# Graph layer on one Trainium2 core: two of six early expert tiles moved from behind the edge loop into it

## What is computed

```python
xf = layernorm(x)                                  # 3125 x 256
gate_logits = xf @ Wg + bg                         # 8 experts
top_w, top_i = top_k(gate_logits, 2)
w = softmax(top_w)                                 # two experts for each node
for e in range(8):                                 # 256 -> 1024 -> 256
    h = gelu(xf @ W1[e] + b1[e])
    out = out + w_dense[:, e:e+1] * (h @ W2[e] + b2[e])
return x + out
```

## Time and profile before

| | |
|---|---|
| median of three runs | 973.71 us (973.17 to 973.80) |
| the profiled execution | 970.97 us |
| its span, first to last instruction | 968.9 us |
| mean granted TensorE clock | 0.916 of full |
| busy: PE, DVE, ACT, POOL | 83%, 55%, 44%, 58% |
| the chain that ended last | PE 39%, POOL 26%, issue 15%, DVE 10%, DMA 6% |

### The profile page before, as it was taken

The page is one execution under the profiler, slowest core; times in us unless marked ns, Lnnn a source line. Parts: engine busy times, 40 slices in busy tenths (PEclk is TensorE's granted clock), DMA queues, the critical chain, the costliest instruction groups (busy, mean ns, idle before and its releaser), DMA issues.

```text
span 968.9 us, 17802 instructions
## 1 busy us (share of the span) xinstructions
PE 801.5 (83%) x4831; PEld 693.5 (72%) x4832; DVE 531.3 (55%) x1485; ACT 424.4 (44%) x1125; POOL 565.6 (58%) x580
## 2 busy tenths in 40 slices
PE   7986676776765557978798777799999999999995
PEld 6885554554554446867687665699999999999994
DVE  6789787887776787667677768741111111111111
ACT  4656433443353235774755662543333333333330
POOL 2077777777777777777777777365333333333331
PEclk8997899779677778997999899799999999999998
DMA  8347554555456445756665674973656656656652
GB/s 237 112 127 236 141 135 137 139 155 139 124 156 196 131 127 150 246 171 190 197 178 145 177 229 116 301 238 62 195 163 184 195 162 190 189 165 191 186 162 22
DMA packets 80183, 162.18 MB, mean 167 GB/s; under 512 B 11569, under 2 KB 46278, under 8 KB 79989
## 3 DMA queue, kind: packets, MB, share of 16 engines
q1 hardware_dynamic: 49029, 91.06, 28.9%
q0 software_dynamic: 30528, 69.83, 28.4%
q10 hardware_dynamic: 560, 0.52, 0.2%
HBM read 144.12 MB, written 17.25 MB: 167 GB/s over the span
## 4 chain that ended last, share of the span: by engine, by line
PE 39%; POOL 26%; issue 15%; DVE 10%; DMA 6%; DVEq 1%; ACT 1%; POOLq 0%; ACTq 0%
POOL gathered L999 24%; PE bank L1714 12%; PE bank L1734 12%; PE bank L1563 4%; PE bank L1380 2%; DMA gathered<-h_table,src_row 2%; DVE gathered L2016 2%; DVE acc L1985 2%; PE bank L1620 2%; DMA out<-one_hot 1%; PE bank L1644 1%; PE bank L1550 1%; DMA w_sb<-in_L_gnn_att_dst 1%; DVEq L1979 1%; PE bank L1702 1%
## 5 line engine op out<-in xcount | busy, mean ns | idle before, releaser
L999 POOL DMA_INDIRECT gathered<-h_table,src_row x416 | 402.2, 967 | 129.0 <-issue 126.0
L1563 PE MATMUL bank<-gathered,one_hot 128*128 128x260 f32 x832 | 248.3, 450 | 133.0 <-DVE acc L1985 131.0
L1563 PEld LDWEIGHTS bank<-gathered,one_hot 128*128 128x128 f32 x832 | 174.8, 221 | 179.3 <-DVE acc L1985 149.5
L1345 ACT ACTIVATE one_hot<-bank,one_hot 128x128 f32<-128x128 f32 x312 | 89.2, 369 | 182.5 <-PE bank L1714 182.5
L1059 POOL DMA_INDIRECT out<-one_hot x39 | 61.2, 1569 | 168.8 <-DMA out<-one_hot 114.4
L1714 PEld LDWEIGHTS bank<-one_hot,acc 128*128 128x128 f32 x1248 | 145.5, 192 | 2.7 <-ACT one_hot L1337 0.8
L1714 PE MATMUL bank<-one_hot,acc 128*128 128x128 f32 x1248 | 145.9, 275 | 0.5 <-ACT one_hot L1337 0.5
L1734 PE MATMUL bank<-w_sb,one_hot 128*128 x624 | 141.1, 379 | 0.0
L2016 DVE TENSOR_TENSOR gathered<-gathered,bank 128x1024 f32<-128x1024 f32 x104 | 127.0, 1221 | 3.5 <-ACT gathered L1203 0.4
L1985 DVE TENSOR_TENSOR acc<-acc,bank 64x260 f32 x208 | 87.9, 423 | 70.1 <-issue 53.5
L1734 PEld LDWEIGHTS bank<-w_sb,one_hot 128*128 128x128 f32 x624 | 115.6, 190 | 14.3 <-issue 0.2
(11 more groups left out here) (363 smaller groups left out, 1009.5 us busy)
## 6 DMA issues: line engine op xcount, KB each, us to landing
acc<-in_L_ffn_W SPq DMA_DIRECT2D x40, 1024.0 KB, 5.1
w_sb<-in_L_ffn_W SPq DMA_DIRECT2D x16, 1024.0 KB, 11.4
w_sb<-key_table SPq DMA_DIRECT2D x52, 256.0 KB, 3.5
gathered<-h_table,src_row POOLq DMA_INDIRECT x416, 3.1
h_table<-acc SPq DMA_DIRECT2D x25, 130.0 KB, 2.2
xs<-in_L_ffn_W SPq DMA_DIRECT2D x3, 1024.0 KB, 11.2
out<-xs SPq DMA_DIRECT2D x5, 512.0 KB
xn_table<-w_sb SPq DMA_DIRECT2D x5, 512.0 KB, 5.3
```

The lines of the kernel that those rows point to most:

```text
L999: pool.indirect_dma_start(gathered[:, r, j, :], None, h_table, bass.IndirectOffsetOnAxis(ap=src_row[:, t:t + 1], axis=0)).then_inc(gather_ ...
L1345: op = act.activation(hiddenT[:, k, g * P:(g + 1) * P], hidden_bank[2 * k + half][:, f * P:(f + 1) * P], ACT.Gelu, bias=b1_slot[:, k, g:g ...
L1563: mm = pe.matmul(sum_bank[r % SUMS][:, 0:ROW], one_hot[:, r, j, :], gathered[:, r, j, :], start=(j == 0), stop=(j == G - 1))
```

## The change

The first two of expert 0's three early tiles run inside the edge loop as tiles 10 and 11 of now NI = 12; four (one of expert 0, three of expert 1) are left behind it (NA = 4). All tiles in the loop begin one group sooner, tile 11 at step 99, so that its narrow is in the last step, 103. The weights of expert 0's first layer are loaded at q = 47 instead of behind the loop. `early_work` does two steps in each group. The dynamic tiles are the same.

```diff
-NA = FIRST * DEPTH
+FA = FIRST * DEPTH
+XA = 2
+NA = FA - XA
...
+NI = NL + XA
-FIRST_TURN = 56
+FIRST_TURN = 55
-FIRST_ROWS = 57
+FIRST_ROWS = 56
-EVENTS = 3 * NL + 1
+EVENTS = 3 * NI + 1
...
-        xg_a = [xs[:, 16 + u, :] for u in range(4)] + [xs[:, 8 + u, :] for u in range(2)]
+        xg_a = [xs[:, 16 + u, :] for u in range(4)] 
...
@@ SP, in the edge loop
+                        if q == 47:
+                            computed(c, 24)
+                            sp.dma_start(b2_first, b2[0:1, :]).then_inc(wa_in, 16)
+                            sp.dma_start(w1_a[0], layer_one(0)).then_inc(wa_in, 16)
...
                         if q == 51:
                             computed(c, 30)
+                            sp.wait_ge(wa_in, c * 48 + 33)
+                            sp.sem_inc(waited, 1)
                             sp.dma_start(w2_a[0], layer_two(0)).then_inc(wa_in, 16)
...
@@ SP, behind it
-                    computed(c, 24)
-                    sp.dma_start(w1_a[0], layer_one(0)).then_inc(wa_in, 16)
...
@@ POOL: early_rows_in, and behind the loop
+                    if u == NL:
+                        pool.wait_ge(early_step, c * EARLY_OPS + EARLY_OPS)
+                        pool.sem_inc(waited, 1)
+                        for k in range(2):
+                            pool.wait_ge(xn_stored[k], c * ((len(BATCHES) + 1 - k) // 2 * 16) + 33)
+                            pool.sem_inc(waited, 1)
...
-                for u in range(4, NA):
-                    read_early(u)
...
-                for u in range(8, NL):
+                for u in range(8, NI):
                     add_rows(u)
...
@@ ACT, step
-                    early_gelu(c, s)
-                    if s == EARLY_AT + 5:
+                    if s == EARLY_AT + 3:
                         act.wait_ge(early_step, c * EARLY_OPS + LIST_OPS + 12)
                         act.activation(powers, powers, ACT.Exp).then_inc(powers_ready, 1)
+                    early_gelu(c, s)
...
@@ PE, in the loop
-                        if part == 1 and u and u % LD == 0:
+                        if part == 1 and u == NL:
+                            other_weights(c, 32)
+                        elif part == 1 and 0 < u < NL and u % LD == 0:
...
+                    if u == NL:
+                        other_weights(c, 48)
...
-                        mm = pe.matmul(y_l, hidden_l[:, g * P:(g + 1) * P], w2_l[:, g, :], start=False, stop=(g == KF - 1))
+                        mm = pe.matmul(y_l, hidden_l[:, g * P:(g + 1) * P], (w2_l if u < NL else w2_a[0])[:, g, :], start=False, stop=(g == KF - 1))
...
@@ PE, behind the last put
-                for u in range(DEPTH, NA):
-                    if u > DEPTH:
-                        early_widen(u, 0)
-                        early_widen(u, 1)
-                    if u + 1 < NA:
-                        if u + 1 == 4:
-                            pe.wait_ge(xga_in[1], 16 * (NA - 4))
-                        early_turn(u + 1)
-                    early_narrow(u - 1, 0)
-                    early_narrow(u - 1, 1)
+                pe.wait_ge(experts_ready, 1)
+                early_narrow(2, 0)
+                early_narrow(2, 1)
...
@@ DVE, step
-                    early_work(c, s)
+                    for k in range(2):
+                        early_work(c, 2 * (s - EARLY_AT) + k)
```

More of the change, by code:

```diff
@@ L77 @@
 EARLY_OPS = LIST_OPS + 30
[L78 removed]
+EVENTS = 3 * NI + 1
 WEIGHTS = 208
[L80 removed]
+MINPAIRS = -(-(2 * N - (NA + NI) * P) // (2 * P))
 SPARE = P
@@ L961, in add_rows @@
                         pool.wait_ge(y_added, u * 16)
-                    pool.indirect_dma_start(out, bass.IndirectOffsetOnAxis(ap=add_l[:, u:u + 1], axis=0),
+                    where = add_l[:, u:u + 1] if u < NL else add_a[:, u - NL:u - NL + 1]
+                    pool.indirect_dma_start(out, bass.IndirectOffsetOnAxis(ap=where, axis=0),
                                             rows_l[u], None, compute_op=ALU.add).then_inc(y_added, 16)
@@ L1210, in rows_out @@
                     products(c, 3 * u + 4)
-                    act.activation(rows_l[u], y_l, ACT.Copy, scale=share_l[:, u:u + 1]).then_inc(scalar_l, 1)
+                    own = share_l[:, u:u + 1] if u < NL else share_a[:, u - NL:u - NL + 1]
+                    act.activation(rows_l[u], y_l, ACT.Copy, scale=own).then_inc(scalar_l, 1)
                 def early_parts(c, s):
@@ L1217, in early_parts @@
                     u, part = (s - FIRST_TURN) // PERIOD, (s - FIRST_TURN) % PERIOD
-                    if part == 0 and 1 <= u <= NL:
+                    if part == 0 and 1 <= u <= NI:
                         rows_out(c, u - 1)
-                    if part == 0 and 0 <= u < NL:
+                    if part == 0 and 0 <= u < NI:
                         products(c, 3 * u + 2)
@@ L1225, in early_gelu @@
                     u, part = (s - FIRST_TURN) // PERIOD, (s - FIRST_TURN) % PERIOD
-                    if part == 2 and 0 <= u < NL:
+                    if part == 2 and 0 <= u < NI:
                         products(c, 3 * u + 3)
-                        at = (LOW + u // LD) * KF
+                        at = (LOW + u // LD) * KF if u < NL else 0
                         for g in range(KF):
@@ L1297, in early_gelu @@
                         g = half * (KF // 2) + f
-                        op = act.activation(hidden_a[:, u % 2, g * P:(g + 1) * P], bank[5 + (2 * u + half) % 3][:, f * P:(f + 1) * P], ACT.Gelu,
-                                            bias=b1_cols[:, u // DEPTH * KF + g:u // DEPTH * KF + g + 1])
+                        op = act.activation(hidden_a[:, u % 2, g * P:(g + 1) * P], bank[5 + (2 * (u + XA) + half) % 3][:, f * P:(f + 1) * P], ACT.Gelu,
+                                            bias=b1_cols[:, (u + XA) // DEPTH * KF + g:(u + XA) // DEPTH * KF + g + 1])
                     op.then_inc(hidden_ready, 1)
@@ L1326, in _ @@
                 shares(8)
-                for u in range(DEPTH, NA):
+                for u in range(3, NA):
                     for half in range(2):
@@ L1513, in weights, with other_weights @@
                     pe.sem_inc(waited, 1)
+                def other_weights(c, count):
+                    pe.wait_ge(wa_in, c * 48 + count + 1)
+                    pe.sem_inc(waited, 1)
                 def early_products(c, s):
@@ L1519, in early_products @@
                     u, part = (s - FIRST_TURN) // PERIOD, (s - FIRST_TURN) % PERIOD
-                    if part == 0 and 1 <= u <= NL:
+                    if part == 0 and 1 <= u <= NI:
                         early_narrow_in(c, u - 1)
-                    if not 0 <= u < NL:
+                    if not 0 <= u < NI:
                         return
@@ L1614, in early_widen @@
                         pe.wait_ge(hidden_ready, 2 * u + half - 2)
-                    if u == DEPTH and half == 0:
+                    if u + XA == DEPTH and half == 0:
                         pe.wait_ge(wb_in, 32)
@@ L2185, in after_step @@
                         dve.sem_inc(waited, 1)
-                    step = s - EARLY_AT
                     if step == 0:
```

74 lines of the change are left out of this document (37 added, 37 removed).

## The result

The changed kernel takes 992.23 us (median of 4 executions, 991.35 to 994.69) against 973.75: ratio 1.0191, 95% interval 1.0168 to 1.0215. Slower, as forecast; 986.8 was too low, the range held it. The profiled execution took 991.76 us with a span of 990.0 us, 21.1 more than the span of before (968.9).

A forecast was written before the change was run, and what follows sets the result against it. POOL bounds the edge loop, PE the tiles from about 704 us; between them PE and POOL's chain of adds arrive together. Terms 1.1 + 5.5 + 3.5 + 1.5 + 1.5 = +13.1 us gave 986.8 us, range 977 to 995.

The forecast's parts named there:

- Covered edits ... All at 0: Weight loads, early list work, early exponential and SP order, all moved sooner, cost 0, with +2 in the range.
- Two gathers on POOL, +1.1: Edge loop: two more tiles' gathers cost POOL 2.5 us, moving the last exponentials by +1.1, between 0 and +2.5.
- The loop's end, +5.5: Loop's end: the twelfth tile's gelus and narrow in series make exponentials to last add 12.3 us instead of 6.8.
- POOL waits for the gelu, +3.5: Behind the loop: add 0 waits for the twelfth gelu, later adds meet weight loads, delaying `put` 0; 0 to +7.
- PE does the same as now: Before the last `put`, PE's work stays as before: widen 0 to 3, narrow 0 and 1.
- A colder PE, +1.5: PE idles 5 us before `put` 0 and restarts slowly once: +1.5, bounds 0 and 2.8.
- Removal worth nothing, +1.5 for the tail: After the routing: two tiles fewer gain nothing because POOL's adds keep their length; contended loads cost +1.5, between 0 and +4.
- Every new wait restarts PE at the lower clock: Rival: waits at `put` 0, first and third dynamic transpose cost 2.8 us each; +20, 993.7 us, chance 0.13.
- Only the loop's end shifts: Rival: adds land undisturbed, `put` 0 waits for nothing, PE stays warm; +6.6, 980.3 us, chance 0.20.
- faster: Rival: earlier weight loads shorten the adds before tile 5's gather, which lands 6.6 us sooner; -2.2, 971.5 us, chance 0.11.
- The signs: Dynamic row gather 10 to 13 us later, POOL waiting 9 us, last sums near 608, PE idle at two places.

The follow-up runs named there:

- run 1: The changed kernel with the early tiles' row gathers one group later in POOL's program, as in the kernel before; 6.3 us faster than the changed kernel.
- run 2: The kernel before with its ten early tiles begun one group sooner, transposes and row gathers, no extra tile; 5.8 us slower than the kernel before.
- 8: The changed kernel with row gathers one group later, adds unwaited and spread, last narrow behind the last sums, two dynamic gathers early; 970.57 us, ratio 0.9965.
- 9: All four edits together, plus early tile 1's widen reading expert 0's weights instead of expert 1's; not faster than the four edits' 970.57 us.
- number 10: All four edits together, plus PE's narrow of early tile 0 ahead of early tile 1's widen; not faster than the four edits' 970.57 us.
- run 11: The kernel before with adds 7, 8 and 9 spread over POOL's weaves and the first early add before tile 0's gather; some 2 us slower.
- run 12: The changed kernel without the two extra loop tiles, first tile at its old place, four early tiles behind; 3.4 us slower than the kernel before.
- Run 4: The changed kernel with the twelfth tile's narrow behind the last edge sums and its rows copy behind the deviations and normalisations; 993.49 us.
- 5: The changed kernel with the row gathers for dynamic tiles 2 and 3 moved behind adds 9 and 10; 5.6 us slower than the changed kernel.
- 7: The changed kernel with adds early and 7 to 11 spread over weaves, two dynamic gathers earlier; last put to dynamic turn 5 38.96 us instead of 51.82.
- run 3: The changed kernel without POOL's waits for the last early tile ahead of the adds; some 2 us less than the changed kernel.

## Why the prediction was right in sign and too low

- **The failed step is "Covered edits ... All at 0".** Beginning one group sooner was costed by what PE, DVE and SP do with it; the row gather on POOL, the engine that bounds the loop, moved ahead of its list. The price is at least one group of POOL's gathers (5.0 us): undoing it gives 6.3 us in run 1, and doing it alone costs 5.8 to 6.6 in run 2, where 3.1 us of the profiled execution's loss lie behind the loop. The trace of the kernel before told it: 344.07 with a wait of 0.40 in the kernel before, 1.28 us after the list's last operation.
- *Two gathers on POOL, +1.1:* neither refuted nor measured. From row gather to A it is 250.2 to 250.9 us in runs 1, 8, 9 and 10 (twelve tiles, gather at group 57), and 249.5, 247.3 and 250.3 in the kernel before and runs 11 and 12 (ten tiles, the same group): the scatter of the three is larger than the term. In runs 1, 8, 9 and 10 the list itself is done 1.5 to 2.5 us later than in the kernel before; why is open (run 11, with the old loop, shows +0.8 too).
- *The loop's end, +5.5:* the series was right, the sum mis-sized: +7.20, in every run with the narrow inside the loop. Left out was the second half of the twelfth tile's widen, which stands on PE ahead of the gelus (the table load waits 1.24 us for it). Run 4 takes bias row, narrow and rows copy out: 5.07 of it.
- *POOL waits for the gelu, +3.5:* half the story; +5.45 (the prediction's own chain of adds gave 3.1, and 3.5 was taken). The adds alone would hold `put` 0 by as much (run 4), but so does a second chain that I denied ("PE does the same as now"): early tile 1 is now one of expert 1, whose first-layer weights go into the accumulators' space and start only after the last scaling (SP issues them at 623.35, behind the stores of the last node tiles). Alone it costs 4.3 us in A to C and 3.4 us of the kernel (run 12).
- *A colder PE, +1.5:* +1.62 in C to D. The half widen behind `put` 0 took 3.39 us instead of 1.96. That the size fits C to D is in part luck: in run 1 `put` 0 waits 2.85 us, the half widen behind it takes 1.96, and C to D is 22.31 as in the kernel before. There the slow stretch comes behind a wait of 1.46 us at the first dynamic tile (half widens of 2.81 and 2.66 us instead of 2.05 and 1.95), and D to E is 53.52.
- *Removal worth nothing, +1.5 for the tail:* right. D to E +0.10, the rest +0.96, and runs 5, 7, 11 and 12 show it from four sides: with seven adds between the last `put` and the first dynamic add 51.5 to 53.8 us, with or without the two tiles; with five adds and the tiles 51.35; with four adds and without the tiles 39.0 (in runs 9 and 10, with more adds delayed, 39.2 and 40.5).
- *Rivals.* "Every new wait restarts PE at the lower clock" lay nearest, at 993.7, but not for its reason. At its three places PE ran a half widen in 3.39 instead of 1.96 us behind a wait of 2.93, the first half widen of a dynamic tile in 2.05 behind 1.41, as in the kernel before, and a narrow in 5.40 instead of 3.62 behind 11.17: 3.2 us in all, where that rival had 8.4. The windows view of the changed kernel shows the granted clock of the stretches with the first and the other two waits, and between them one without a wait (busy us of PE, PEld, DVE, ACT, POOL; clock, a mean of the two levels 1.2 and 2.4 GHz; DMA, GB/s):

```profile
645.00:652.00 7.00, 4.07 (x26) 4.08 (x26) 1.70 (x2) 2.71 (x11) 5.95 (x7) 0.81 0.71 216
652.00:672.00 20.00, 20.00 (x162) 19.55 (x162) 7.63 (x16) 8.54 (x32) 11.80 (x11) 0.98 0.69 208
672.00:700.00 28.00, 14.89 (x101) 13.37 (x100) 3.36 (x15) 5.23 (x18) 12.06 (x9) 0.89 0.47 113
```

The last narrow lies just behind the last row: from 700 to 706 us the granted clock was 0.67. The Trainium skill's rule (TensorE: Matmul & The Clock Gate, HAM oscillation) agrees as far as the bursts behind the waits of 2.93 and 11.17 us start slow. That every wait restarts PE slow is not what the runs show, and the length of the wait alone does not tell: behind 1.41 us here PE is not slow, behind 1.46 us in run 1 it is, and behind 2.85 us there it is not. The Trainium skill (ScalarE: Activation LUTs, What ACT_TABLE_LOAD costs) adds a drain of about 1.38 us to a switch of tables. It does not show here: the loads end at 605.16 and 613.71, the next activations begin at 605.17 and 613.73, and the second load begins 0.02 us behind the copy before it. *Only the loop's end shifts* fell with B to C, *faster* with D to E, which did not shrink.
- *The signs.* POOL's wait ahead of add 0 (10.75 us, 9 forecast) and PE's waits at `put` 0 and the third dynamic transpose came as said. The last edge sums end at 613.6 us instead of near 608, and the first row gather of the dynamic tiles comes 20.0 us later (673.83) instead of 10 to 13: both carry the group that POOL lost and the mis-sized terms.

Open: the list wait was not tried with only the operations that the gather needs, nor number 10 with its adds placed so that no weave stands behind a long link, nor the adds spread without the two row gathers moved.

## What to carry to other kernels

Before work is taken out of a stretch, look for the engine whose program has a chain of waits through that stretch; if it arrives together with the busy one, the work is filling, and the removal pays only after the chain is shortened (0 of 14.5 us here, 12.9 once three of seven adds stood ahead of the stretch and two row gathers earlier among the rest). When a step starts earlier, check on the engine that bounds the loop each wait in front of it, and how many microseconds lie between its releaser and its start now: a margin of nothing becomes a whole group. Two chains that end at one point are found only by edits made together.

## What was not expected of the hardware

An add into the output costs 4.0 us from issue to issue when little else moves, and over twice that beside loads of 1 MB: in run 3 adds 2, 3 and 4 come at 610.29, 614.33 and 618.34 (33 GB/s from 610 to 618 us), in run 4 add 3 comes 9.1 us after add 2 (624.53, 633.64; 366 GB/s from 624 to 633 us). That stretch, not the issue on POOL (1.57 us in both), makes the place of these adds worth more than their number.
